# A layernorm, mixture-of-experts and neighbour-attention block: biases written into PSUM ahead of the products instead of multiplied in

## What is computed

```
x = x + 0.5 * ffn(layernorm(x))        # 8 experts, the best two of each row
x = x + attn(layernorm(x))             # 16 heads of 16, each row sees its two neighbours and itself
x = x + 0.5 * ffn(layernorm(x))        # the same weights again

ffn(x):  gates = softmax(x @ Wg + bg); best two, rescaled to sum 1
         out = sum over the two of gate_e * (x @ We[e] + be[e])
attn(x): xp = x @ Wp.T + bp; q, k, v = xp @ Wq.T + bq, ... ; softmax over 3 neighbours; out @ Wo.T + bo
```

## Time and profile before

| | before |
|---|---|
| median of 3 runs | 1142.07 us (1140.99 to 1143.32) |
| profiled execution | 1144.01 us |
| its span, first to last instruction | 1142.1 us |
| mean granted TensorE clock | 0.976 |
| full steps (both stages) | 28 |
| from the logits of step 7 to those of step 30 | 747.3 us, 32.49 us a step |

### The profile page before, as it was taken

How to read it: one execution, slowest core, us unless ns; L and a number is a source line. 1 busy time by engine, 2 the same in 40 slices (tenths; PEclk the granted TensorE clock), 3 DMA queues, 4 the chain that set the end, 5 groups by cost and what they waited for, 6 DMA issues and landing times.

```text
span 1142.1 us, 18095 instructions
## 1 busy us (share of the span) xinstructions
PE 1075.7 (94%) x5523; PEld 902.0 (79%) x5523; DVE 961.0 (84%) x2679; ACT 492.6 (43%) x1117; POOL 714.1 (63%) x954
## 2 busy tenths in 40 slices
PE   4898799999999999999999999999999999998775
PEld 3677588888888888888888888888888888887553
DVE  3558688989988999889888998898889888988873
ACT  3253344444444444444444445344444354443331
POOL 2366457666766667667667676676766766664343
PEclk9799899999999999999999999999999999999998
DMA  5001000000000000000000000000000000000000
GB/s 161 10 20 41 16 1 20 19 19 20 19 19 15 6 19 19 20 20 19 20 18 7 15 20 19 20 20 19 20 10 11 20 19 20 10 10 10 10 9 19
DMA packets 12583, 23.06 MB, mean 20 GB/s; under 512 B 2212, under 2 KB 5812, under 8 KB 12488
## 3 DMA queue, kind: packets, MB, share of 16 engines
q1 hardware_dynamic: 9240, 13.37, 3.3%
q0 software_dynamic: 3248, 8.54, 2.7%
HBM read 12.47 MB, written 8.39 MB: 18 GB/s over the span
## 4 chain that ended last, share of the span: by engine, by line
PE 81%; DVE 9%; SPq 3%; DMA 2%; issue 2%; ACT 2%; POOL 0%; POOLq 0%; DVEq 0%; ACTq 0%
PE ffn_bank L890 18%; PE ffn_bank L892 18%; PE ffn_bank L891 18%; PE tr_bank L919 4%; PE tr_bank L931 4%; PE mix_bank L890 4%; PE mix_bank L892 4%; PE mix_bank L891 4%; SPq L245 2%; DVE chain_sum L647 1%; PE mix_bank L956 1%; PE tr_bank L890 1%; PE tr_bank L892 1%; DMA we_raw<-in_L_ffn_We 1%; PE tr_bank L891 1%
## 5 line engine op out<-in xcount | busy, mean ns | idle before, releaser
L890 PE MATMUL ffn_bank<-we_hi,T_hi 128*128 128x512 f32 x1024 | 416.1, 406 | 7.0 <-DVE chain_sum L647 2.8
L892 PE MATMUL ffn_bank<-we_hi,T_lo 128*128 128x512 f32 x1024 | 404.4, 395 | 0.0
L891 PE MATMUL ffn_bank<-we_lo,T_hi 128*128 128x512 f32 x1024 | 403.3, 394 | 0.0
L335 POOL TENSOR_TENSOR chain_sum<-chain_sum,we_raw 128x512 f32<-128x512 f32 x128 | 165.8, 1295 | 185.5 <-DVE chain_sum L647 185.5
L449 ACT ACTIVATE we_raw<-ffn_bank,gate 128x256 f32<-128x256 f32 x512 | 211.0, 477 | 141.4 <-PE ffn_bank L892 141.2
L890 PEld LDWEIGHTS ffn_bank<-we_hi,T_hi 128*128 128x128 f32 x1024 | 195.3, 191 | 49.5 <-issue 8.1
L892 PEld LDWEIGHTS ffn_bank<-we_hi,T_lo 128*128 128x128 f32 x1024 | 194.6, 190 | 43.1
L891 PEld LDWEIGHTS ffn_bank<-we_lo,T_hi 128*128 128x128 f32 x1024 | 195.4, 191 | 36.0
L412 ACT CAST T_hi<-tr_bank 128x512 fp32r<-128x512 f32 x128 | 74.9, 589 | 123.4 <-PE tr_bank L919 123.4
L647 DVE SCALAR_TENSOR_TENSOR chain_sum<-ffn_bank,gate,base 128x256 f32<-128x256 f32 x128 | 61.2, 478 | 72.5 <-POOL base L327 45.7
L647 DVE SCALAR_TENSOR_TENSOR chain_sum<-ffn_bank,gate,chain_sum 128x256 f32<-128x256 f32 x256 | 110.7, 473 | 9.2 <-PE ffn_bank L892 9.1
(11 more groups left out here) (134 smaller groups left out, 1887.6 us busy)
## 6 DMA issues: line engine op xcount, KB each, us to landing
out_x<-y SPq DMA_DIRECT2D x31, 256.0 KB
we_raw<-in_L_ffn_We SPq DMA_DIRECT2D x2, 1024.0 KB, 14.7
x_in<-in_L_attn_x,x_row POOLq DMA_INDIRECT x60
x_in<-in_L_attn_x SPq DMA_DIRECT2D x2, 256.0 KB, 7.6
moved_qk<-qk SPq DMA_DIRECT2D x4, 124.0 KB
w_raw<-in_L_attn_Wq SPq DMA_DIRECT2D x1, 256.0 KB, 2.8
w_raw<-in_L_attn_Wk SPq DMA_DIRECT2D x1, 256.0 KB, 2.9
w_raw<-in_L_attn_Wv SPq DMA_DIRECT2D x1, 256.0 KB, 3.8
```

Source lines behind the costliest of these rows:

```text
L335: nc.gpsimd.tensor_tensor(chain_sum[:, f, t], chain_sum[:, f, t], scaled[:, f, t, 1], ALU.add).then_inc(done, 1)
L890: nc.tensor.matmul(dest, hi[:, t, k, :], w_hi_[:, k, c0:c1], start=(k == 0), stop=False)
L891: nc.tensor.matmul(dest, hi[:, t, k, :], w_lo_[:, k, c0:c1], start=False, stop=False)
L892: last = nc.tensor.matmul(dest, lo[:, t, k, :], w_hi_[:, k, c0:c1], start=False, stop=(k == KB - 1 and not more))
```

## The change

Biases are no longer multiplied. ScalarE copies a row that every partition holds into a PSUM bank before TensorE's product, and the product adds onto it.

* `be` is loaded into all partitions as `be_all` (128 x 2048 f32, 1 MB in SBUF, one DMA on GpSimd's queue). `seed_bank(b, ...)` copies 512 columns of it into FFN bank b. Each of the 64 x 2 tiles needs its four banks seeded anew (the last tile's need not be), and `ffn_step` waits for `seeded[b]` alone. The seed of bank 0 stands behind the reading of bank 0, those of banks 1 and 2 behind the reading of bank 2, and that of bank 3 behind the reading of bank 0 **of the next tile**.
* Two seeds of 128 x 512 a pair for Q/K (`seed_step`, after LN2's normalisation) take the place of L991.
* `gate_parts`, `gateT_step`, `bias_step`, `base_step` go on all engines; the chain starts from x itself, so x has three buffers (`XIN` is 3), and the gather waits for FFN1's chain.
* Matmuls into these banks never start a group. Once, in the setup, a matmul writes each FFN bank; the folded bias row's product (L1011) is widened and now stands behind that. The setup of the bias rows on VectorE goes.
* TD's transpose moves from behind FFN2's tile 1 bank 0 to behind bank 1.

The core of the diff:

```diff
+        be_all = sb("be_all", [PART, E * D])
-        x_in = sb("x_in", [PART, 2, 2, D])
+        x_in = sb("x_in", [PART, XIN, 2, D])
...
-                    await_(pool, base_done[FFN1], (s + 1).times(1, 1))
+                    pool.wait_ge(chain_done[FFN1], s.times(8, 5))
...
+            def seed_bank(b, f, n, t):
+                if (f, n, t) != tile_order[-1]:
+                    if b % 2:
+                        act.wait_ge(chain_done[f], 8 * n + 4 * t + b + 1)
+                    else:
+                        act.wait_ge(scaled_done[f], 4 * n + 2 * t + b // 2 + 1)
+                    nc.scalar.copy(ffn_bank[b][:, :], be_all[:, b * BANK:(b + 1) * BANK]).then_inc(seeded[b], 1)
...
                     last.then_inc(scaled_done[f], 1)
+                    if b == 0:
+                        if tile_no[here] > 0:
+                            seed_bank(3, *tile_order[tile_no[here] - 1])
+                        seed_bank(0, *here)
+                    else:
+                        seed_bank(1, *here)
+                        seed_bank(2, *here)
...
+            def seed_step(n):
+                for t, (read, value) in enumerate(((v_copied, n.const), (qk_copied, 2 * n.const))):
+                    await_(act, read, value)
+                    nc.scalar.copy(mix_bank[t][:, :], bqkv[:, 0:2 * D]).then_inc(qk_seeded, 1)
...
-                nc.tensor.matmul(mix_bank[t][:, :], ones[:], bias_qk[:], start=False, stop=True).then_inc(qk_done, 1)
...
+            pe.wait_ge(setup_act, 8)
+            pe.wait_ge(setup_dve, 3)
+            for b in range(4):
+                last = nc.tensor.matmul(ffn_bank[b][:, :], wqkv_hi[:, 0, 0:PART], wqkv_hi[:, 0, 0:BANK], start=True, stop=True)
+            last.then_inc(columns_written, 1)
...
-                    if not drained:
-                        ffn_step(FFN2, s - 4, s, 0, range(1, 4))
-                    ffn_step(FFN2, s - 4, s, 1, range(0, 2 if drained else 1))
+                    ffn_step(FFN2, s - 4, s, 0, range(3 if drained else 0, 4))
+                    ffn_step(FFN2, s - 4, s, 1, range(0, 2))
```

More of the change, by code:

```diff
@@ L217, in gates_of @@
             return slice(0 if (s + 1).within(PAIRS) else 2, 4 if (s - 4).within(GROUPS) else 2)
+        tile_order = [(f, s - 4 * f, t) for s in range(PAIRS + 4) for f in range(NF) for t in range(2)
+                      if 0 <= s - 4 * f < PAIRS]
+        tile_no = {tile: no for no, tile in enumerate(tile_order)}
         def gate_round(f, n):
@@ L228, in _ @@
                     w_loaded if w < 4 else wp_loaded, 16)
-            for n in range(2):
+            for n in range(XIN):
                 sp.dma_start(x_in[:, n, :, :], x_tiles[:, 2 * n:2 * n + 2, :]).then_inc(x_loaded[n], 16)
@@ L496, in _ @@
             nc.scalar.copy(bv_wide[:], tr_bank[0][:, 0:KB * PART].rearrange("p (k n) -> p k n", k=KB)).then_inc(setup_act, 1)
+            act.wait_ge(be_loaded, 16)
+            act.wait_ge(columns_written, 1)
+            for b in range(4):
+                nc.scalar.copy(ffn_bank[b][:, :], be_all[:, b * BANK:(b + 1) * BANK]).then_inc(seeded[b], 1)
             def body(s):
@@ L642, in chain_step @@
                     if b == 1:
-                        start = (base[:, f, t], scaled[:, f, t, 0, 0])[j]
+                        start = (x_in[:, n.const % XIN, t] if f == FFN1 else x2[:, n.slot, t], scaled[:, f, t, 0, 0])[j]
                     else:
@@ L731, in x2_step @@
                 dve.wait_ge(x1_bo_done, a.times(1, 2))
-                await_(dve, base_done[FFN2], (a - 1).times(1))
+                await_(dve, chain_done[FFN2], 8 * (a.const - 2) + 5)
                 for t0, t1, at in runs(slots_of(a, 1)):
@@ L884, in _, with product @@
             last.then_inc(setup_pe, 1)
-            def product(dest, i, n, t, w_hi_, w_lo_, c0, c1, more=False):
+            def product(dest, i, n, t, w_hi_, w_lo_, c0, c1, first=True):
                 hi, lo = halves(i, n)
                 for k in range(KB):
-                    nc.tensor.matmul(dest, hi[:, t, k, :], w_hi_[:, k, c0:c1], start=(k == 0), stop=False)
-                    nc.tensor.matmul(dest, hi[:, t, k, :], w_lo_[:, k, c0:c1], start=False, stop=False)
-                    last = nc.tensor.matmul(dest, lo[:, t, k, :], w_hi_[:, k, c0:c1], start=False, stop=(k == KB - 1 and not more))
+                    nc.tensor.matmul(dest, hi[:, t, k, :], w_hi_[:, k, c0:c1], start=(first and k == 0), stop=False, skip_group_check=not first)
+                    nc.tensor.matmul(dest, hi[:, t, k, :], w_lo_[:, k, c0:c1], start=False, stop=False, skip_group_check=not first)
+                    last = nc.tensor.matmul(dest, lo[:, t, k, :], w_hi_[:, k, c0:c1], start=False, stop=(k == KB - 1), skip_group_check=not first)
                 return last
@@ L1070, in body @@
                 if (s - 4).within(GROUPS):
-                    ffn_step(FFN2, s - 4, s, 1, range(2 if drained else 1, 4))
+                    ffn_step(FFN2, s - 4, s, 1, range(2, 4))
                 if s.within(PAIRS) and not filling:
```

207 lines of the change are left out of this document (49 added, 158 removed).

## The result

The changed kernel takes **1201.63 us** (median; 1198.32 to 1203.05), the kernel before in the same comparison 1142.7 us: a ratio of 1.0506, 95% interval 1.0488 to 1.0525. It is 5.1% slower. The prediction was 1208 us.

What follows compares the result with a forecast made beforehand. TensorE's work and the chain VectorE, exponential, reading of bank 0 were taken to bound together. 1144 + 27 x 1.85 (steps) + 15 (clock) + 8 (start, filling) - 2 (draining) = 1215, lowered to 1208 us; range 1140 to 1246.

Steps and rivals of the forecast that it cites:

- What bounds: Full step before the change, 32.33 us: TensorE's work and the chain VectorE, exponential, reading of bank 0 end together.
- TensorE's saving: Per full step, two Q/K bias matmuls, four expert-bias matmuls and the gates' transpose go from TensorE: 1.04 us.
- A seed: ScalarE's 128 x 512 copy into PSUM: 0.5 us each, bounds 0.3 and 0.65, 18 a step.
- The seed of bank 3: FFN2's tile 1: seed queued behind exponential, cast and bank 0's reading; bank 3 starts 2.9 us later than TensorE could.
- The step: Full step with the late bank 3: 34.2 us, 1.9 us more than 32.33.
- The clock: Low granted clock after the new wait at bank 3, in one step of three: 27 x 0.6 = 15 us.
- Start and filling: Larger loads, later folded bias product and seed waits, less setup and gate waits: +8 us, bounds 0 and +14.
- Draining: Final steps, bound by VectorE's chain, a seed replacing a transpose and a product: -2 us, bounds -6 and +6.
- The sum: Whole kernel: 1144 + 27 x 1.85 + 15 + 8 - 2 = 1215, lowered to 1208 us.
- A: Rival: the chain slips but x_bo misses VectorE's products; step 33.1 us, kernel 1170 us; chance 0.18.
- B: Rival: faster, VectorE's head start reaches the exponential and TensorE bounds; step 31.5 us, kernel 1126 us; chance 0.15.
- C: Rival: TensorE's clock falls in nearly every step; kernel 1246 us; chance 0.12.

Runs made afterwards that it cites:

- the last version: Changed kernel with reading of FFN2's tile 1 bank 0 and seeds of banks 3 and 0 before the exponential, x_bo between FFN2's sums: 1116.52 us.
- The last two runs: Changed kernel with bank 0's reading and seeds of banks 3 and 0 before the exponential: x_bo beside the products 1145.1 us, between FFN2's sums 1116.52 us.

## Why the prediction was right, point by point

- **What bounds.** The chain over x2, the scores and the exponential beside TensorE's own work: right. The version without FFN seeds has all of TensorE's saving and still has steps of 32.16 us, since the first product waits for the reading behind the exponential. The trace of before has a test of it, too. In three of its 25 steps the last operation ahead of the exponential (L694) takes 0.85 us and not 0.26, and the first product, which waits in no other of them, waits for the reading; the step lasts 33.1 us and not 32.5, with the clock granted at 1.00. DVE and PE:

```profile
457.69 0.85 DVE L694 TENSOR_TENSOR score<-score,most 128x96 f32<-128x96 f32 x1
```
```profile
460.22 0.47 PE L890 MATMUL ffn_bank<-we_hi,T_hi 128*128 128x512 f32 x1 [0.73 <-ACT we_raw L449]
```

  An exponential 0.6 us later makes the step 0.6 us longer: there was no slack.
- **TensorE's saving, 1.04 us a step.** Where nothing makes TensorE wait, in the last version, most steps last 31.5 us; before, 32.3 and 32.5 in turn. That is 0.9 us. (The three terms that I named add up to 1.02, not 1.04.)
- **A seed, 0.5 us.** Two in a row take 1.1 us, so 0.55 each. The mean of one row, by the list of ScalarE's groups: from PSUM to SBUF, from SBUF to PSUM, and from SBUF to SBUF:

```profile
L457 ACT COPY qk<-mix_bank 128x512 f32<-128x512 f32 x64 | 37.6, 588 | 49.4 <-PE mix_bank L855 49.3
L446 ACT COPY mix_bank<-bqkv 128x512 f32<-128x512 f32 x64 | 34.9, 574 | 0.0
L454 ACT COPY qk<-moved_qk 128x512 f32<-128x512 f32 x2 | 1.2, 614 | 0.0
```

  with 599 ns for the FFN seeds. The Trainium skill, page "ScalarE: Activation LUTs", section "ACT is a hardware spline evaluator", says that ScalarE reaches PSUM sooner than SBUF. With the same source and shape the trace agrees in direction, by little and on two copies alone: 574 and 599 ns into PSUM, 614 ns into SBUF. The seed was not near my lower bound of 0.3, and leaving the sum at 0.5 was right. ScalarE ends at 745.6 us, where I wrote near 780.
- **The seed of bank 3.** x2 at T0 + 0.20 (predicted 0.22), the wait for the idle copy gone (0.17 us), the products 2.96 us in the form that I had reckoned with (2.95) and 3.17 in the other, the exponential at T0 + 10.92 and 11.08 (10.92), bank 3 at T0 + 13.12 in the second form (13.06). Beside the last version it starts 2.9 us late, as predicted. The wait of about 0.5 us that I put at tile 0's bank 3 is 0.42 us at tile 1's bank 1, and its reason is another one: not LN2's normalisation ahead of it but the products. The last two runs show that the collision would cost 29 us even with bank 3 in time. Here the later wait takes that in, as the text said of its 0.5 us.
- **The step, 34.2 us.** 34.3 and 34.5 in turn, 2.0 us more than the 32.3 and 32.5 of before, and not 1.9.
- **The clock, 15 us: mis-sized.** Four of the 25 steps last about 1.6 us longer than their neighbours, 6.5 us together. The 25 steps hold 53.8 us more than before: 25 times 1.97 is 49.3, the clock adds 6.5, and 2 go off for the three slow steps of the kernel before, which are not the clock's (see the first point). The term that was too large is "one step in three", and with it the thought that the length of the wait decides alone (see the end): it was one in six.
- **Start and filling, +8.** +9.3. The first FFN product comes at 41.53 us, 8.5 later than before (33.07), and the run with the start mended gains 6 to 9 us.
- **Draining, -2.** -5.5, inside its bounds.
- **The sum.** Predicted 71 us over the profiled execution of before, 57.6 measured. Of the 13 us between them 8 are the clock's term, 3.5 the draining's and 3 the steps', against 1 on the other side for the start. My step down to 1208 "for the seed's lower bound" had no ground in the end; it only happened to go the right way.
- **The rivals.** A, the missed collision, came out as an experiment: I gave it 1170 us, and the run that moves x_bo took 1171.3, with 33.2 and 33.4 us for its plain steps where I had 33.1; what the clock and the second meeting of VectorE and GpSimd added there, a shorter filling took off, and that was luck. B did not happen and its condition, x2 free of the projection, is not met in any run. C did not happen: the clock fell in four of 25 steps.

## What to carry to other kernels

Work given to an engine that is busy for 43% can cost 5% all the same: look up behind which wait of that engine's queue each added instruction stands, and when its result is due. Here the sum over the queue gave the loss as 71 us where it was 57.6, and moving that one instruction ahead of the late one gave most of it back; with the neighbour's collision gone as well, the same idea was 2.6% faster than the kernel before. And when an operation ahead of a late one goes, look what its neighbours run into: by the order of its list, GpSimd's sum x_bo had been kept off VectorE's products only by the sum that the change removed. A small wait that a larger one takes in is still to be followed to its cause, because it is the next bound once the larger one is gone.

## What the runs showed of the hardware

- VectorE and GpSimd collide also where VectorE's operation is tiny. In the version with x_bo moved, DVE's first maximum of 128 x 32 takes 0.18 us and its second, of the same shape, 1.28 us; POOL's sum of 1.29 us had started 0.05 us earlier:

```profile
636.45 0.18 DVE L677 TENSOR_TENSOR most<-score 128x32 f32<-128x32 f32 x1
636.66 1.28 DVE L679 TENSOR_TENSOR most<-most,score 128x32 f32<-128x32 f32 x1
```
```profile
636.61 1.29 POOL L321 TENSOR_TENSOR chain_sum<-chain_sum,we_raw 128x512 f32<-128x512 f32 x1 [2.33 <-DVE chain_sum L634]
```

  The tiny operation waits for about the whole of the large one. The Trainium skill says so, page "SBUF — State Buffer", section "Who interferes with whom", and the traces agree. It stands on the chain to the exponential in this kernel; no run moved it. The operation behind it, of 128 x 96, meets `pool_sum` in the same way, but only in some steps: 0.84 us in place of 0.26 in 3 of the 25 steps of the kernel before and in 9 of those with x_bo moved.
- The products paid 1.1 us for x_bo in both their forms (1.86 to 2.96, 2.07 to 3.17), less than the 1.28 us that x_bo takes alone; x_bo's own row is 1.74 us beside the first form and 1.48 beside the second.
- The length of a wait alone does not tell whether TensorE's clock falls. In the changed kernel the wait at tile 1's bank 3 is 1.94 or 1.95 us in each of the 25 steps, and the clock fell behind only four of them. With x_bo moved it fell behind none of 16 waits of 1.47 to 1.62 us and behind five of nine of 2.19 us, so the longer waits were hit more often, and none of these lengths decides. Of two waits of the changed kernel, the clock fell behind this one and not behind the one at 624.75 (windows: length, busy of five engines, granted clock, DMA share, GB/s):

```profile
485.57 0.50 PE L853 MATMUL ffn_bank<-we_hi,T_hi 128*128 128x512 f32 x1 [1.94 <-ACT ffn_bank L417]
```
```profile
485.50:491.00 5.50, 5.43 (x19) 4.38 (x20) 3.31 (x8) 4.12 (x10) 2.37 (x3) 0.69 0.00 0
624.00:630.00 6.00, 5.25 (x25) 4.30 (x26) 4.22 (x11) 6.00 (x14) 2.50 (x4) 1.00 0.01 3
```

  What the four have in common stays open.
